# Two residuals moved into weight matrices in a four-layer post-norm kernel on Trainium2

## What is computed

```
x = LN(x + scan_attention(x))             # layer 0: gated running sums, then out_w, out_b
x = LN(x + (x @ W[idx] + b[idx]))         # layer 1: one of 8 matrices, chosen by logits and noise
x = LN(x + metric_attention(x))           # layer 2
x = LN(x + mlp(x))                        # layer 3: gated 128 -> 512, two 512 -> 512 with gelu, 512 -> 128

# layer 2, for each of 16 heads with 8 channels and each sequence
proj   = x @ projection
pm     = proj @ metric                    # symmetric 8 x 8 for each head
dots   = pm @ proj.T                      # no softmax
nudged = dots @ proj                      # = pm @ (proj.T @ proj)
out    = nudged @ mixer_w.T + mixer_b
```

## Time and profile before

| | us |
|---|---|
| median of 3 runs | 222.52 |
| lowest and highest | 221.82, 222.86 |
| profiled execution, whole | 223.1 |
| its span, first to last instruction | 221.2 |
| PE busy in the span | 192.3 |
| DVE busy | 153.9 |
| ACT busy | 112.7 |
| POOL busy | 79.4 |

### The profile page before, as it was taken

One profiled execution on the slowest core, in us unless ns is written; L12 is line 12 of the kernel. 1 busy time (PEld: TensorE's weight loads), 2 busy tenths in 40 slices (PEclk: granted clock), 3 DMA queues, 4 the chain that ended last, 5 costly groups with the idle time before them and its releaser, 6 DMA issues.

```text
span 221.2 us, 3102 instructions
## 1 busy us (share of the span) xinstructions
PE 192.3 (87%) x972; PEld 145.2 (66%) x972; DVE 153.9 (70%) x385; ACT 112.7 (51%) x172; POOL 79.4 (36%) x67
## 2 busy tenths in 40 slices
PE   6659886978996999999999999999997989999940
PEld 6128664466873767788877868897774767666820
DVE  0378957897978679978868899777896227671143
ACT  2497923123027764322298732225996346895630
POOL 4020006121011902751345739233469332354401
PEclk9997998899999999999999999999999999999985
DMA  5995020100000010000000100000001000001001
GB/s 132 316 431 216 15 59 1 47 0 0 3 0 0 0 52 1 0 0 3 0 0 1 47 0 0 0 0 0 0 3 49 0 0 0 0 3 47 0 3 50
DMA packets 6125, 8.19 MB, mean 37 GB/s; under 512 B 480, under 2 KB 4832, under 8 KB 5728
## 3 DMA queue, kind: packets, MB, share of 16 engines
q1 hardware_dynamic: 6112, 8.02, 10.7%
HBM read 6.97 MB, written 1.05 MB: 36 GB/s over the span
## 4 chain that ended last, share of the span: by engine, by line
issue 34%; PE 23%; POOL 19%; DVE 11%; ACT 5%; DMA 4%; SPq 1%; POOLq 1%; DVEq 0%
PE c_bank L803 10%; POOL rstd L292 5%; POOL hid_even_low L308 5%; POOL hid_odd_low L308 4%; DMA xt<-x_tok 4%; POOL res L287 4%; PE y_bank L771 3%; PE b_bank L790 3%; DVE state L564 3%; DVE normed_lent L549 2%; PE b_bank L936 2%; DVE read L572 1%; ACT hid L415 1%; DVE stats L532 1%; PE b_bank L785 1%
## 5 line engine op out<-in xcount | busy, mean ns | idle before, releaser
L292 POOL TENSOR_TENSOR rstd<-varied,power 128x4 f32<-128x4 f32 x16 | 17.8, 1114 | 78.4 <-DVE varied L542 78.4
L564 DVE TENSOR_TENSOR_SCAN state<-rep_bank,keep 128x256 f32<-128x256 f32 x64 | 39.8, 670 | 4.6 <-PE rep_bank L763 4.5
L771 PEld LDWEIGHTS y_bank<-attend_pack,read 128*128 128x128 f32 x256 | 33.0, 198 | 13.2 <-DVE read L572 11.5
L771 PE MATMUL y_bank<-attend_pack,read 128*128 128x128 f32 x256 | 36.0, 287 | 5.4 <-DVE read L572 4.8
L308 POOL TENSOR_TENSOR hid_even_low<-hid,hid_even_high 128x512 fp32r<-128x512 f32 x16 | 20.4, 1283 | 34.4 <-ACT hid L415 24.8
L413 ACT ACTIVATE hid_even_high<-c_bank,scales_pack 128x512 fp32r<-128x512 f32 x16 | 11.0, 689 | 27.7 <-PE c_bank L803 27.7
L415 ACT ACTIVATE hid<-c_bank,scales_pack 128x512 f32<-128x512 f32 x32 | 21.8, 682 | 0.0
L572 DVE TENSOR_TENSOR read<-state,query 128x512 f32<-128x512 f32 x32 | 21.4, 679 | 0.0
L803 PE MATMUL c_bank<-hid_even_high,hidden_rounded 128*128 128x512 f32 x64 | 19.7, 414 | 0.6 <-ACT gate L390 0.6
L803 PE MATMUL c_bank<-hid_even_low,hidden_rounded 128*128 128x512 f32 x64 | 18.9, 400 | 0.4 <-DVE hid_even_low L595 0.4
L803 PE MATMUL c_bank<-hid_odd_high,hidden_rounded 128*128 128x512 f32 x64 | 19.2, 412 | 0.0
(11 more groups left out here) (129 smaller groups left out, 359.8 us busy)
## 6 DMA issues: line engine op xcount, KB each, us to landing
hidden_pack<-hidden SPq DMA_DIRECT2D x2, 1024.0 KB, 11.8
attend_pack<-attend SPq DMA_DIRECT2D x1, 1152.0 KB, 7.7
xT_lent<-x_chan SPq DMA_DIRECT2D x4, 256.0 KB, 8.6
xt<-x_tok SPq DMA_DIRECT2D x4, 256.0 KB, 3.2
mlp_pack<-mlp SPq DMA_DIRECT2D x1, 768.0 KB, 9.6
out<-xT_lent SPq DMA_DIRECT2D x3, 256.0 KB, 2.3
metric_pack<-metric SPq DMA_DIRECT2D x1, 384.0 KB, 13.2
project_pack<-project SPq DMA_DIRECT2D x1, 256.5 KB, 2.7
```

The costliest lines, as they stand in the source:

```text
L292: nc.gpsimd.tensor_tensor(rstd[n][:], varied[n][:], power[:], ALU.pow).then_inc(ln_rstd[n], 1)
L564: ins = nc.vector.tensor_tensor_scan(state[:, e % STATES, at], rep_bank[e % 2][:, at], keep[:, bass.ds(a * T + s * SEQ, SEQ)], 0.0, ALU.ad ...
L771: ins = nc.tensor.matmul(y1_bank[:, tile(j)], read[:, e % READS, tile(j)], out_w_rep_sb[:, e, :], start=(e == 0 and j == 0), stop=False, s ...
```

## The change

Two residuals stop being additions and become part of a weight matrix.

- Layer 1: once, POOL makes `passed_w = chosen_w + identity` (128 x 128), and L790 multiplies with `passed_w`, so that the bank holds `x + x @ W`. The bias `chosen_b` is added by `norm_sum` on DVE in place of `res1`, through a view that repeats it for each of the four tiles.
- Layer 2: `moved` is gone. The matrix `metric_proj` (made once, the transposed product of what `proj_metric` was) is multiplied with `mixed` (128 x 256, two sequences), and DVE adds the identity to the result, giving `through`, one 128 x 128 matrix for a sequence. The last product of the layer is `x2T` with `through`. The bias `mixer_b` is added in `norm_sum`.

With this, `residual(1, ...)` and `residual(2, ...)` leave POOL in every group (eight instructions of 128 x 512), together with the waits for `norm_out` in front of them. ACT loses the copy `moved`. PE loses L922 and gains one product over 256 columns, which stands behind attend 5. DVE gains `through` (128 x 256, from `b4_bank`) behind its last `read` of the step.

```diff
@@ gpsimd step @@
                 if b is not None:
                     inverse_std(1, b)
-                    if first(b):
-                        pool.wait_ge(loaded["metric"], 16)
-                    if a is not None:
-                        pool.wait_ge(ln_out[1], nth(b, NT, NT))
-                        residual(2, b, res2, normed[1], mixer_b_sb)
                 if c is not None:
                     for layer, chunks in POOL_GELUS:
                         for m in chunks:
                             low_gelu(c, layer, m)
-                        if layer == 1 and a is None and b is not None:
-                            pool.wait_ge(ln_out[1], nth(b, NT, NT))
-                            residual(2, b, res2, normed[1], mixer_b_sb)
                 if b is not None:
                     inverse_std(2, b)
                 if a is not None:
                     inverse_std(0, a)
-                    pool.wait_ge(ln_out[0], nth(a, NT, NT))
                     if first(a):
                         pool.wait_ge(chosen_loaded, 32)
-                    residual(1, a, res1, normed[0], chosen_b)
+                        pool.wait_ge(loaded["metric"], 16)
+                        nc.gpsimd.tensor_tensor(passed_w[:], chosen_w[:], ident_sb, ALU.add).then_inc(passed_ready, 1)
@@ scalar step @@
-                    move(b, 5, moved, b4_bank, b4_free)
...
-                    move(b, 7, mixed[:].rearrange("p s c -> p (s c)"), b4_bank, b4_free, GS * P)
+                    move(b, 6, mixed[:].rearrange("p s c -> p (s c)"), b4_bank, b4_free, GS * P)
@@ vector norm_sum @@
+                if n in (1, 2):
+
+                    if n == 1 and first(group):
+                        dve.wait_ge(chosen_loaded, 32)
+                    view = "p (j c) -> p j c"
+                    nc.vector.tensor_tensor(total[n].rearrange(view, j=NT), bank_[:].rearrange(view, j=NT),
+                                            (chosen_b[:], mixer_b_sb)[n - 1].unsqueeze(1).to_broadcast([P, NT, P]),
+                                            ALU.add).then_inc(summed, 1)
@@ vector step, behind the last read_state @@
+                if b is not None:
+                    dve.wait_ge(b_ready, nth(b, B4 + B5, 7))
+                    nc.vector.tensor_tensor(through[:], b4_bank[:, 0:GS * P].rearrange("p (s c) -> p s c", s=GS),
+                                            ident_sb.unsqueeze(1).to_broadcast([P, GS, P]),
+                                            ALU.add).then_inc(b4_free, 1)
@@ tensor step @@
-                    per_tile(b5_bank, x1T, lambda j: chosen_w[:]).then_inc(b_ready, 1)
+                    per_tile(b5_bank, x1T, lambda j: passed_w[:]).then_inc(b_ready, 1)
...
-                    nc.tensor.matmul(proj_bank[0][:, 0:P], proj_t_sb, metric_sb, start=True,
+                    nc.tensor.matmul(proj_bank[0][:, 0:P], metric_sb, proj_t_sb, start=True,
                                      stop=True).then_inc(pm_ready, 1)
...
-                    nc.tensor.matmul(b4_bank[:], proj_metric[:], x2T[:], start=True, stop=True).then_inc(b_ready, 1)
...
+                if b is not None:
+                    pe.wait_ge(b4_free, nth(b, B4, 3))
+                    if first(b):
+                        pe.wait_ge(pm_copied, 1)
+                    nc.tensor.matmul(b4_bank[:, 0:GS * P], metric_proj[:], mixed[:].rearrange("p s c -> p (s c)"),
+                                     start=True, stop=True).then_inc(b_ready, 1)
                 if c is not None and (a is not None or b is None):
                     hidden(c, 2, 1)
...
                     pe.wait_ge(b4_free, nth(b, B4, 4))
-                    per_tile(b5_bank, moved, lambda j: mixed[:, j // TPS, :]).then_inc(b_ready, 1)
+                    per_tile(b5_bank, x2T, lambda j: through[:, j // TPS, :]).then_inc(b_ready, 1)
```

More of the change, by code:

```diff
@@ L128, in build @@
         chosen_w, chosen_b = sb("chosen_w", [P, P]), sb("chosen_b", [P, P])
-        proj_metric = sb("proj_metric", [P, P])
+        passed_w = sb("passed_w", [P, P])
+        metric_proj = sb("metric_proj", [P, P])
         xT, xt = lent["xT"], sb("xt", [P, T])
@@ L154, in build @@
         x3T_parts = [sb(f"x3T_{which}", [P, T], F32R) for which in ("high", "low")]
-        res1, res2, res3 = sb("res1", [P, T]), sb("res2", [P, T]), sb("res3", [P, T])
-        heads, moved = xT_lent[0], xT_lent[1]
+        res3 = sb("res3", [P, T])
+        heads = xT_lent[0]
+        through = sb("through", [P, GS, P])
         gram, mixed = sb("gram", [P, GS, P]), sb("mixed", [P, GS, P])
@@ L198, in build @@
         o_free = [sem("o0_free"), sem("o1_free")]
+        passed_ready = sem("passed_ready")
         weights_ready = sem("weights_ready")
@@ L432, in step @@
                     act.wait_ge(pm_ready, 1)
-                    nc.scalar.copy(proj_metric[:], proj_bank[0][:, 0:P]).then_inc(pm_copied, 1)
+                    nc.scalar.copy(metric_proj[:], proj_bank[0][:, 0:P]).then_inc(pm_copied, 1)
                     projections(range(2 * PROJECTIONS, 3 * PROJECTIONS))
@@ L524, in norm_sum @@
                 dve.wait_ge(ready, value_)
-                dve.wait_ge(res_ready[n], nth(group, 1, 1))
-                nc.vector.tensor_tensor(total[n][:], bank_[:], (res0, res1, res2, res3)[n][:],
-                                        ALU.add).then_inc(summed, 1)
+                if n in (1, 2):
[5 more added lines that the diff above has]
+                                            ALU.add).then_inc(summed, 1)
+                else:
+                    dve.wait_ge(res_ready[n], nth(group, 1, 1))
+                    nc.vector.tensor_tensor(total[n][:], bank_[:], (res0, None, None, res3)[n][:],
+                                            ALU.add).then_inc(summed, 1)
                 dve.wait_ge(summed, sums)
@@ L662, in step @@
                 if b is not None:
-                    dve.wait_ge(b_ready, nth(b, B4 + B5, 6))
+                    dve.wait_ge(b_ready, nth(b, B4 + B5, 5))
                     nc.vector.tensor_tensor(gram[:], b5_bank[:, 0:GS * P].rearrange("p (s c) -> p s c", s=GS),
@@ L874, in step @@
                     if first(b):
-                        pe.wait_ge(chosen_loaded, 32)
+                        pe.wait_ge(passed_ready, 1)
                     else:
@@ L942, in step @@
                 if b is not None:
-                    pe.wait_ge(b4_free, nth(b, B4, 3))
                     pe.wait_ge(b5_free, nth(b, B5 - 2, 2))
```

## The result

| | before | after |
|---|---|---|
| median, us | 222.69 | 233.01 |
| lowest and highest, us | 221.82, 223.12 | 230.28, 235.06 |
| runs | 4 | 4 |
| profiled execution, us | 223.1 | 233.58 |
| its span, us | 221.2 | 231.8 |

The changed kernel takes 1.043 times as long as the one before, with an interval of 1.033 to 1.053. It is slower, as forecast, but by 10.3 us where 6.5 were forecast, and 233.0 lies above the upper end of the range, 231.6. Each experiment is compared with runs of the kernel before on its own chip, whose median was 222.8 to 223.7.)

A forecast was written before the change was run, and what follows sets the result against it. PE's stream of work plus its waits was taken to bound the loop. Terms 4.6 + 0.5 + 0.2 + 0 + 0.4 + 0.8 = +6.5 gave 229.0 us on the median, range 225.5 to 231.6.

The forecast's parts named there:

- direction, mechanism and place: In the loop, POOL's low parts would block `norm_out`, about 4 us for four pieces, PE resuming 2.75 late; kernel slower.
- The turn's price without the clock: Each loop turn 2.3 us longer, from 1.9 late at L936 plus 0.4 for the new product; two turns +4.6.
- the 0.54 of waiting in `hidden(c, 2, 0)`: Between attend 3 and L936 in each turn, a 0.54 us wait for the last low parts would vanish.
- The new product over 256 columns: In each loop turn, PE's added product would cost half of L922, 0.43 us.
- the clock: Half clock after PE's new gap in the loop: +0.8 us in all, at most 1.1 in a turn, at least 0.
- the loop's entry: First low part meets `norm_out` instead of residual 1: set at 0, between -0.6 and +0.6 us.
- rival 2: Half clock in both loop turns and longer at the second step's start: +8.9, 231.4 us; chance 0.20.
- +7.9 by its rule: By the skill page's warning on pauses, both loop turns fall to half clock: 5.7 + 2.2 = +7.9 us.
- the second step's start: One blocked `norm_out` piece, +1.0 us, taken as +0.5 for half clock there; rest of that step +0.2.
- `through` and the serial chain: `through` free in the loop, last product 0.4 late in the second step; behind the loop, net +0.4 us.
- Rival 1: Low parts and `norm_out` do not meet in the loop: two turns -1.9, 221.2 us; chance 0.08.
- Rival 3: PE catches up about 2 us in a loop turn: sum about +1.3 to +3, 224 to 225.5 us; chance 0.10.

The follow-up runs named there:

- Experiment 3: Kernel before, all residuals and products kept, with only POOL's low parts moved ahead of the norm 1 wait and residual 2 in the loop: 232.36 us, ratio 1.035.
- 1: Changed kernel with POOL again waiting for norm 1's output before its low parts inside the loop, no residual computed: 226.85 us, ratio 1.016.
- kernel 2: Changed kernel with POOL waiting for norm 1's output in the loop and also for norm 0's output: 222.25 us, ratio 0.996.
- experiment 6: Changed kernel with idle PE products before transposes of norm 0 (start, loop's entry) and norm 1 (in and behind the loop): 229.42 us, ratio 1.032.
- kernel 10: Kernel before with idle PE products in the gaps at the start and behind the loop: 222.12 us, ratio 0.995.
- experiment 4: Changed kernel with four idle PE products before each of the first three transposes of norm 1, in the loop only: 232.71 us, ratio 1.041.
- experiment 5: Changed kernel with POOL waiting for every norm's output before its low parts, in the step behind the loop too: 224.38 us, ratio 0.997.
- Kernel 9: Kernel 2 plus idle PE products in the gaps at the start and behind the loop: 221.07 us, ratio 0.989.

## Why the prediction was right and where it was wrong

**Right: direction, mechanism and place.** The price was forecast from the earlier trace rows, the same pieces in the other order behind the loop. In the changed loop `norm_out` took 3.79 (4.00 was taken over from there), PE waited about 1 us three times, POOL's low parts took 3.70 (3.73), and PE resumed 2.7 and 2.8 late at replicate 4 (2.75) in turn 1 and 2. Experiment 3 shows that the order alone does it, and 1 and 2 that a wait undoes it. The Trainium skill, "SBUF — State Buffer", section "SBUF: two separate sides", says that of DVE in its two-port mode and GpSimd the one that comes second stands fully blocked for a whole instruction. These runs agree: one piece ends per low part, 1.22 apart. No view shows which mode the pieces ran in, and no run separates a shared port from another cause of the same alternation, so that the port itself is taken from there and not shown here.

**The turn's price without the clock: 2.3 forecast, 2.6 measured.** The step that was off is the 0.54 of waiting in `hidden(c, 2, 0)` that the early low parts would save. It came from the chain's row of L936 (139.31) set against the timeline's attend 3 (136.01). In one view, the timeline, L936 starts at 139.14, so attend 3 to L936 is 3.13 there. With the low parts early it is 2.85 in experiment 6 (143.82 - 140.97), and the saving is 0.28. That is 0.26 of the missing 0.3. The forecast took one difference from two views whose times for the same product are 0.17 apart. It did so once more, less visibly: the last product of layer 2 in the second step, 60.27 by the chain, starts at 60.13 in the timeline. The new product over 256 columns cost 0.4 as forecast: by the gram product the second turn of experiment 6 is 2.20 late against before, by its end 2.63.

**Wrong: the clock.** This is the largest miss: by the traces it is 2.4 us, and without it the result would lie inside the range. The prediction gave it +0.8, "about one of the two turns", and 0 at the loop's entry. In the trace of after it is 0.4 and 1.7 in the turns (46.20 and 46.85 against 45.79 and 45.19 in experiment 6), where 1.1 was to be the most in a turn, and 1.4 at the entry; net of what half clock cost before, it is 3.2 (experiments 6 and 10). Both turns fell, the second for 6.8 us and not for one stretch of 3.3, and so did the loop's entry. The choice was between two rows, one gap that fell and one that stayed at 1.00. I took the mean of them, though the new gap was longer than either. The row that stayed at 1.00 was no reason for hope: that same place behind the loop kept full clock in the profile of after and fell in that of experiment 4, with the same blocked norm around it. A single profiled execution shows that a gap can pass, not that it does. In rival 2, which put half clock into both turns and gave 231.4, most of this stood, though it was 1.6 short as well; its chance of 0.20 looks too low. The Trainium skill, "TensorE: Matmul & The Clock Gate", section "Why this matters for your kernels", warns of pauses between bursts of matmuls; for this sum it was nearer the truth (+7.9 by its rule) than my reading of the one row, and the traces agree with it in both turns of after and of experiment 3, but not behind the loop, where before and after kept 1.00 with PE busy 1.01 of 2.8 us.

**Wrong: the loop's entry.** It was set at 0, between -0.6 and +0.6, on the ground that the first low part meets `norm_out` instead of residual 1. The meeting is there, with 2.06 for the pieces instead of 1.11, but I had not followed it to PE. PE was already waiting for those pieces, so it resumed 0.7 later (0.9 without half clock in either kernel, 1.86 - 0.95 by experiments 6 and 10), and half clock followed with another 1.4 up to the start of turn 1, of which a wait of before took 0.5 back. It is the same mechanism as in the loop, one piece of it, and the same question (who waits for the norm?) would have found it.

**Right for the wrong amounts, before the entry.** At the second step's start the passed product is 1.8 late. Some 0.7 of that was there already, from a longer stretch of half clock at the kernel's start (13.0 to 19.8 instead of 16.4 to 19.8), which is no part of the change. The 1.8 shrinks to 0.9 by the last product of layer 2, since that stretch of the second step now runs at full clock, where it had 0.50 before. The forecast (+0.7 in all) comes near, but by another sum, and that is luck. At full clock in both kernels (experiments 6 and 10) the blocked norm costs 1.02 there, the +1.0 of the forecast before it took half off for the clock, and 0.95 is left by the last product (59.19 against 58.24).

**`through` and the serial chain.** The new link waits where it was said to and nowhere else. In the second step:

```profile
60.98 1.16 PE L800 MATMUL b_bank<-through,x1T 128*128 128x128 f32 x8 [1.03 <-DVE through L679]
```

and behind the loop, where the two links and the saved L922 leave +0.3 (forecast +0.4):

```profile
189.81 0.70 PE L963 MATMUL b_bank<-mixed,metric_proj 128*128 128x256 f32 x2 [0.46 <-ACT mixed L382]
191.02 1.16 PE L800 MATMUL b_bank<-through,x1T 128*128 128x128 f32 x8 [0.52 <-DVE through L679]
```

**The account.** Forecast 4.6 + 0.5 + 0.2 + 0 + 0.4 + 0.8 = 6.5. Measured by the trace: turns without the clock 5.2; behind the loop 0.3; up to the last product of layer 2 0.9; the entry's blocked norm 0.7. That is 7.1, and the span grew by 10.6; the 3.5 that are left are half clock at the entry and in the turns. The 0.9 ahead of the entry has some clock of its own, in both directions. The pair without it (experiments 6 and 10) gives 5.2 + 0.4 + 0.95 + 0.9 = 7.4, where the forecast had 5.7 without its clock term: 0.6 more in the turns, 0.9 at the entry and 0.25 in the second step. So of the 4.1 that the forecast missed of the span, 2.4 are the clock (3.2 against 0.8), 0.9 the entry, and the rest the turns and the second step.

**Rivals.** Rival 1 (no new blocking) is out: `norm_out` took 3.79, not under 2. Rival 3 (the loss is absorbed) is out: PE caught up 0.57 in a turn, 2.77 to 2.20 by the gram product of experiment 6, not 2.

**What stays open.** Why a stretch of half clock lasts 3.4 us in one case and 6.8 in another, and which executions of a kernel fall at a gap, isn't settled; runs of one kernel spread by up to 6.0 us (experiment 5), and one execution of the kernel before took 313.02 us at a mean granted clock of 0.558. Also not tried: POOL's low parts ahead of `rstd`, where they would meet other work of DVE.

## What to carry to other kernels

A wait in front of work that is being removed may be what keeps two engines from blocking each other. Before taking it out, ask which instructions now come together, and look in the same trace for a place where they already do: the price stands there (the earlier trace rows against the earlier trace rows), and one line that waits gives it back. Follow each such meeting to who waits for the blocked result: the same wait was worth 2.6 us a turn in the loop, a microsecond and a stretch of half clock at its entry, and nothing behind it. And a new gap of PE costs the gap plus, very likely, a stretch of half clock behind it; one execution that kept its clock over such a gap is no evidence that the next will.

## What the runs showed that I had not expected

- The clock's share varies by execution. The four runs of after have mean granted clocks of 0.965, 0.956, 0.948 and 0.930, and times of 230.3, 232.4, 233.6 and 235.1 us, in that order. In the loop of after half clock began while PE was doing single transposes between its waits: in the 3.4 us ahead of each fall (91.5 to 94.9 and 135.9 to 139.3) it was busy 0.98 and 1.49 us.
- With one gap filled, half clock turned up at another place: the profile of experiment 4 has 1.00 all through the loop and two stretches at 0.50 behind it, where the profile of after has none before 228 us.
- Whether filled gaps make a kernel steadier is not shown. Kernel 9 spreads over 1.7 us in 6 runs, and kernel 2, the same without idle products, over 5.0 in 10; but kernel 10 spreads over 3.1 in 12, and the kernel before on the same chip, without the one execution of 313.02, over 3.5 in 16.
- Where low parts and norm pieces met, only DVE paid. The three low parts took 3.70 in the loop, 1.23 each, less than the 4.66 of before, where they had met `read` and not the norm.
